# Postponed-layernorm ViT layer: a third buffer for h times C, transposes first in TensorE's step, the second image's projections over free banks, dummy matmuls at the end

## The chip, the cores and the metric

One core of one Trainium2 chip. The metric is the device time of one execution in microseconds (us), as the median of three runs. One of the executions was profiled; the trace and its rows are from that one.

## The reference, cut to what matters

Four images of 1024 tokens with 64 features go through three blocks in fp32: retention (scores weighted with a fixed 1024x1024 matrix, PReLU), a selective state scan, and a two-layer mixture of experts, with a layer norm behind the second and the third.

```python
# retention, per image
q, k, v = x @ Wq + bq, x @ Wk + bk, x @ Wv + bv
y = ((d_gamma * (q @ k.T)) @ v) @ Wo + bo
h = where(y >= 0, y, prelu_a * y)
# state scan: 128 channels, 16 states
x_main, x_gate = split(h @ W_in + b_in)
x_conv = silu(x_main @ W_conv + b_conv)
B, C = split(x_conv @ W_bc + b_bc);  dt = softplus(x_conv @ W_dt + b_dt)
h_state = exp(dt * A) * h_state + dt * B * x_conv      # along the 1024 tokens
y = (h_state * C).sum(states)
h = layernorm(h + (y * silu(x_gate)) @ W_out + b_out)
# experts: each group of 64 tokens has one routed expert of 16, and a shared one
f = relu(h @ Wi.T + bi)
for l in 0, 1:  f = relu(shared_l(f) + expert_l(f) + f)
h = layernorm(h + f @ Wo.T + bo)
```

## The kernel before, in words

Everything is written out by hand, engine by engine, with semaphores; no scheduler reorders anything. Features or channels lie on the partitions and tokens along the free axis, in fp32. PSUM is divided into five named parts: `acc_y` (two banks, the sum of h times C over the states, transposed), `slot` (two banks, named `decay` in the trace), `work` (two banks), `acc_r` (one) and `tail` (one).

Every engine runs the same double loop: phases p = -1 to 5, and in each 16 steps n, one per state of the scan (`PHASES`, `step_of`). In a phase, image p is scanned (state number k = 16 p + n), image p + 1, called head, goes through retention in steps 0 to 8 and through its conv, gate, B, C and step-size products in steps 9 to 13, and image p - 1 goes through its layer norms and expert products (`last_part`, 19 steps, the last three in the next phase). In steps 11 to 14 the queries, keys and values of the image after head are made. So phase -1 is the start, with image 0's retention alone, phases 0 to 3 scan images 0 to 3, and the rest is image 3's end alone.

One state k of the scan goes through four engines:
- ScalarE writes the decay exp(dt A) into `slot` (`fill_slot`, L653 through `decay_exp` L633), once scan k - 1 has read it.
- u times B: for 11 of the 16 states GpSimd makes it (`ub`, L811, three buffers); for states 0, 4, 8, 10 and 14 VectorE does it in PSUM (L907), where ScalarE has copied u (L651).
- VectorE scans along the tokens into one of three h buffers (L919).
- GpSimd multiplies h with the broadcast row C (`hc`, L820, two buffers, `weigh`).
- TensorE transposes hc in eight 128x128 pieces, adding them in `acc_y` (`states_out`, L500), two steps later.

In GpSimd's step n stand hc(k-1) and then ub(k+1). The B and C rows come from DRAM, 512 KB each as each partition gets a copy, through SyncE's queue: three b_row and four c_row buffers, loaded three steps ahead (`load_b`, `load_c`); the group weights of the expert products (`load_group`) and the output stand in the same queue.

TensorE's step n holds, in this order: tail parts marked EARLY; scores(n+1) and retention(n) for n < 8; at step 9 the conv product (L468, needs the finished h of retention) and the gate product (L477, needs ScalarE to have read the conv product out of `work`); at step 10 the products out of xc for B and C (L484) and for the step sizes (L490); then states_out(k-2); then a side projection (steps 11 to 14: q, first keys, values, second keys, each through `acc_r`, evicted by ScalarE, L667 to L673); then scores(0) of the next image at step 15; then tail parts marked LATE. The expert products of an image are four such parts (L563 for the bias, L568 for 8 groups): layer 1 for the two halves at steps 8 and 9, layer 2 at 11 and 12. VectorE evicts them (L972) in the steps that DVE_TAIL names. In the last image's end TensorE is alone, and `tail` and the first bank of `work` alternate.

At the start TensorE first multiplies zeros (L391), then the folded weights (L394 to L396), the queries, keys and values of image 0 (L404, L400, L410), then scores and retention.

## Time and profile before

| | us |
|---|---|
| median of three runs (lowest, highest) | 401.34 (395.81, 404.02) |
| the profiled execution | 401.9 |
| its span from first to last instruction | 400.1 |
| busy: TensorE matmuls / weight loads | 304.3 / 174.2 |
| busy: VectorE, ScalarE, GpSimd | 251.7, 175.0, 262.2 |
| mean granted TensorE clock, share of full speed | 0.805 |

The profile names the engines PE (TensorE matmuls), PEld (its weight loads), DVE (VectorE), ACT (ScalarE), POOL (GpSimd), SP (SyncE). A row of the groups of instructions gives, for a line and an operation, how often it ran, its busy time and mean duration, and the idle time of its engine just before it with what ended that. Busy matmul time is modelled, as matmuls are pipelined. The granted clock has two levels, 1.2 and 2.4 GHz, shown as 0.50 and 1.00 of full speed; a value between them is a mean over a stretch. An fp32 matmul appears as two records.

### The profile page before, as it was taken

Reading aid. Unit: us, or ns where it says so; the run is one execution under the profiler, and the core shown is the slowest. Engines: PE = TensorE matmul, PEld = TensorE weight load, DVE = VectorE, ACT = ScalarE, POOL = GpSimd, SP = SyncE. Lnnn points to the kernel's source line nnn. Section 1 sums busy time; section 2 is a strip of 40 time slices with the busy share of each in tenths; the row PEclk is TensorE's granted clock in tenths of the full one; section 3 lists DMA queues with packets and bytes.
Section 4 is the critical chain, followed back from the end, with each engine's and each line's share of the span. In section 5 each row is a group of like instructions: output and inputs, shape, how many; then the busy total and the mean of one; then the engine's idle time right before and its main releaser. Section 6 shows DMA issues by size and latency. Waiting matters only on the chain.

```text
span 400.1 us, 4140 instructions
## 1 busy us (share of the span) xinstructions
PE 304.3 (76%) x1368; PEld 174.2 (44%) x1368; DVE 251.7 (63%) x221; ACT 175.0 (44%) x209; POOL 262.2 (66%) x116
## 2 busy tenths in 40 slices
PE   8995779756686889699796997667655786956793
PEld 5321413322352434365742444456443375731771
DVE  3556268977388799752949988649667667640020
ACT  2019233347744336746363356863553533333003
POOL 0062219993998899746778799486999979840000
PEclk9999558995987999758689999896759586696556
DMA  7930837776569789953657998765699998313201
GB/s 262 422 116 13 313 111 280 242 244 240 183 223 260 274 270 328 274 193 141 209 185 228 273 298 302 240 214 202 220 302 283 323 317 280 107 26 98 61 2 26
DMA packets 42998, 85.87 MB, mean 215 GB/s; under 512 B 7904, under 2 KB 24800, under 8 KB 42720
## 3 DMA queue, kind: packets, MB, share of 16 engines
q1 hardware_dynamic: 42576, 84.43, 63.6%
q10 hardware_dynamic: 400, 1.17, 1.0%
q8 instruction: 11, 0.18, 0.2%
q14 instruction: 11, 0.09, 0.1%
HBM read 75.62 MB, written 1.57 MB: 193 GB/s over the span
## 4 chain that ended last, share of the span: by engine, by line
PE 35%; POOL 22%; DVE 19%; issue 10%; ACT 8%; DMA 3%; SPq 1%; POOLq 1%; DVEq 0%; ACTq 0%
POOL ub L811 12%; DVE h L919 11%; POOL hc L820 10%; PE acc_y L500 7%; PE tail L568 5%; PE acc_r L457 3%; PE work L448 3%; DVE decay L907 2%; DVE mixed L937 2%; DMA b_row<-bc_dram 2%; PE tail L522 2%; PE work L568 2%; PE tail L553 1%; PE tail L544 1%; PE work L490 1%
## 5 line engine op out<-in xcount | busy, mean ns | idle before, releaser
L820 POOL TENSOR_TENSOR hc<-h,c_row 128x1024 f32<-128x1024 f32 x64 | 151.8, 2372 | 55.5 <-PE acc_y L500 42.2
L919 DVE TENSOR_TENSOR_SCAN h<-decay,ub 128x1024 f32<-128x1024 f32 x44 | 100.8, 2290 | 49.1 <-POOL ub L811 41.6
L811 POOL TENSOR_TENSOR ub<-u,b_row 128x1024 f32<-128x1024 f32 x44 | 103.9, 2362 | 14.3 <-DMA b_row<-bc_dram 14.3
L633 ACT ACTIVATE decay<-delta,neg_a 128x1024 f32<-128x1024 f32 x44 | 49.2, 1119 | 96.6 <-DVE h L919 96.6
L500 PEld LDWEIGHTS acc_y<-pack,hc 128*128 128x128 f32 x512 | 68.1, 162 | 51.4 <-issue 30.3
L500 PE MATMUL acc_y<-pack,hc 128*128 128x128 f32 x512 | 81.9, 312 | 8.8 <-POOL hc L820 8.6
L937 DVE TENSOR_TENSOR mixed<-gam,work 128x512 f32<-128x512 f32 x56 | 35.6, 676 | 17.3 <-PE work L448 16.5
L919 DVE TENSOR_TENSOR_SCAN h<-decay_own,decay 128x1024 f32<-128x1024 f32 x20 | 45.7, 2286 | 0.7
L448 PE MATMUL work<-q,kT 64*128 64x512 f32 x112 | 35.5, 713 | 13.8 <-DVE mixed L937 11.0
L568 PEld LDWEIGHTS tail<-f,group_w 128*128 128x128 f32 x224 | 39.3, 263 | 1.0
L457 PE MATMUL acc_r<-mixed,v_sb 128*64 128x512 f32 x128 | 37.2, 662 | 1.7 <-DVE mixed L937 1.7
L568 PE MATMUL tail<-f,group_w 128*128 128x64 f32 x224 | 38.0, 344 | 0.0
L907 DVE TENSOR_TENSOR decay<-decay,b_row 128x1024 f32<-128x1024 f32 x20 | 24.6, 1230 | 14.3 <-ACT decay L651 14.3
L651 ACT ACTIVATE decay<-u 128x1024 f32<-128x1024 f32 x20 | 20.5, 1027 | 28.1 <-DVE h L919 28.1
L448 PEld LDWEIGHTS work<-q,kT 64*128 64x128 f32 x112 | 9.4, 204 | 31.9 <-DVE mixed L937 23.1
L633 ACT ACTIVATE decay_own<-delta,neg_a 128x1024 f32<-128x1024 f32 x20 | 22.7, 1136 | 0.0
L972 DVE TENSOR_SCALAR f<-tail 128x512 f32<-128x512 f32 x14 | 9.6, 686 | 17.1 <-PE tail L568 16.8
L563 PE MATMUL tail<-onehot,bias_w 96*128 96x512 bf16 x14 | 7.0, 503 | 15.8 <-DVE f L972 12.6
L797 POOL TENSOR_TENSOR expert_w<-expert_w 128x2048 f32<-128x2048 f32 x2 | 9.0, 4518 | 15.2 <-DMA expert_w<-routed_w 15.2
L457 PEld LDWEIGHTS acc_r<-mixed,v_sb 128*64 128x64 f32 x128 | 6.6, 141 | 28.0 <-issue 18.9
L732 ACT ACTIVATE ln_q<-tail,b_c 128x512 f32<-128x512 f32 x8 | 5.4, 678 | 26.6 <-PE tail L544 26.6
L400 PE MATMUL acc_r<-x_in,pack 128*128 128x512 f32 x12 | 9.0, 843 | 7.7 <-ACT q L667 6.5
(134 smaller groups left out, 297.3 us busy)
## 6 DMA issues: line engine op xcount, KB each, us to landing
b_row<-bc_dram SPq DMA_DIRECT2D x64, 512.0 KB, 5.0
c_row<-bc_dram SPq DMA_DIRECT2D x64, 512.0 KB, 5.1
group_w<-expert_w SPq DMA_DIRECT2D x64, 128.0 KB, 3.8
gam<-gammaT SPq DMA_DIRECT2D x8, 512.0 KB, 10.3
expert_w<-routed_w SPq DMA_DIRECT2D x1, 2048.0 KB, 18.1
x_in<-xT SPq DMA_DIRECT2D x4, 256.0 KB, 5.7
out<-res SPq DMA_DIRECT2D x8, 128.0 KB, 3.1
pack<-packed ACTq DMA_DIRECT2D x1, 788.0 KB, 6.6
```

The source lines that it names most:

```text
L448: nc.tensor.matmul(pair[:, i * HALF:(i + 1) * HALF], kT[D * i:D * i + D, j * P:(j + 1) * P], q2[D * i:D * i + D, :], start=True, stop=True ...
L457: mm = nc.tensor.matmul(acc_r[D * i:D * i + D, :], v_sb[:, j, :], mixed[:, j % 2, i * HALF:(i + 1) * HALF], start=(j == 0), stop=(j == TIL ...
L500: mm = nc.tensor.matmul(acc_y[:, c * P:(c + 1) * P], hc[:, k % 2, c * P:(c + 1) * P], ident, start=(n == 0 and c % 4 == 0), stop=(n == STA ...
L568: mm = nc.tensor.matmul(bank[:, (g % 8) * GROUP:(g % 8 + 1) * GROUP], group_w[:, g, layer, :], f[:, g * GROUP:(g + 1) * GROUP], start=Fals ...
L633: nc.scalar.activation(target, delta[:, b % 2, :], ACT.Exp, scale=neg_a[:, n:n + 1])\
L651: nc.scalar.activation(slot[:, :], u[:, b % 2, :], ACT.Copy).then_inc(u_copied, 1)
L811: nc.gpsimd.tensor_tensor(ub[:, j % 3, :], u[:, b % 2, :], b_row[:, k % 3, :], ALU.mult)\
L820: nc.gpsimd.tensor_tensor(hc[:, k % 2, :], h[:, k % 3, :], c_row[:, k % 4, :], ALU.mult)\
L907: nc.vector.tensor_tensor(slot[:, :], slot[:, :], b_row[:, k % 3, :], ALU.mult).then_inc(ub_own, 1)
L919: nc.vector.tensor_tensor_scan(h[:, k % 3, :], factor, term, 0.0, ALU.mult, ALU.add).then_inc(scan_done, 1)
L937: nc.vector.tensor_tensor(mixed[:, j % 2, at], gam[:, j, at], pair[:, at], ALU.mult).then_inc(read, 1)
L972: nc.vector.tensor_scalar(f[:, i * HALF:(i + 1) * HALF], bank[:, :], 0.0, None, ALU.max)\
```

## The change

- hc has three buffers in place of two, c_row three in place of four; C rows are loaded two steps ahead in place of three. The hc of state k waits for the transposes of k - 3.
- TensorE's step: states_out comes right behind scores and retention. The conv product follows it at step 9, the products out of xc at step 10 and the side projections too; the gate product is last in step 9, behind the LATE parts.
- The projections of the second image (made while image 0 is head) no longer alternate with ScalarE in `acc_r`: queries go to `acc_r`, both key halves to the two banks of `slot`, values to `acc_r`; VectorE evicts all four. ScalarE's first use of `slot` waits for that.
- Start: the folded weights come behind the keys, image 0's values behind scores(0, 0).
- Dummy matmuls of 256 columns into `acc_r` (or `slot`) that nobody reads: two at step 8 of phase -1; four ahead of each of the last two states_out; in image 3's end as WARM_AT says.
- VectorE evicts the second half of expert layer 1 at step 11 in place of 10.

```diff
-DVE_TAIL = {2: USE_YT, 3: USE_YT + 1, 6: USE_VAR1, 8: USE_L1, 10: USE_L1 + 1, 12: USE_L2, 13: USE_L2 + 1, 16: USE_VAR2}
+DVE_TAIL = {2: USE_YT, 3: USE_YT + 1, 6: USE_VAR1, 8: USE_L1, 11: USE_L1 + 1, 12: USE_L2, 13: USE_L2 + 1, 16: USE_VAR2}
...
+WARM_AT = {2: 1, 4: 2, 5: 4, 7: 1, 12: 1, 14: 2, 15: 4}
...
-        c_row = sb("c_row", [P, 4, T])
+        c_row = sb("c_row", [P, 3, T])
...
-        hc = sb("hc", [P, 2, T])
+        hc = sb("hc", [P, 3, T])
...
-                if k >= 4:
-                    sp.wait_ge(hc_ready, k - 3)
+                if k >= 3:
+                    sp.wait_ge(hc_ready, k - 2)
...
-                        load_c(k + 3)
+                    if scanned(k + 2):
+                        load_c(k + 2)
...
+            def keep_warm(bank, times):
+
+                for _ in range(times):
+                    nc.tensor.matmul(bank[:, 0:2 * INNER], gam[:, 0, 0:P], gam[:, 0, 0:2 * INNER], start=True, stop=True)
...
+                folded_weights()
+
+            def first_values():
                 pe.wait_ge(s_wvo, 1)
                 values(slot[:, 0:HALF]).then_inc(first_full, 1)
+
+            def next_projections():
+
+                pe.wait_ge(side_read, 1)
+                pe.wait_ge(s_x, 32)
+                queries(acc_r).then_inc(next_full, 1)
+                pe.wait_ge(slot_read, 10)
+                keys(0, slot[:, 0:HALF]).then_inc(next_full, 1)
+                keys(1, slot[:, HALF:T]).then_inc(next_full, 1)
+                pe.wait_ge(next_read, 1)
+                values(acc_r).then_inc(next_full, 1)
...
-                    if head is not None:
-                        if n + 1 < TILES:
-                            scores(head, n + 1)
-                        if n < TILES:
-                            retention(head, n)
-                        if n == 9:
-                            conv_product(head)
-                            gate_product(head)
-                        if n == 10:
-                            from_xc(head)
+                    if head is not None and n + 1 < TILES:
+                        scores(head, n + 1)
+                    if head is not None and n < TILES:
+                        retention(head, n)
+                    if p == IMAGES and n < 2:
+                        pe.wait_ge(side_read, side_use(IMAGES - 1, SIDE_BC) + 1)
+                        keep_warm(acc_r, 4)
                     if scanned(k - 2):
                         states_out(k - 2)
-                    if following is not None and n in SIDE_AT:
+                    if head is not None and n == 9:
+                        conv_product(head)
+                    if head is not None and n == 10:
+                        from_xc(head)
+                    if head == 0 and n == 11:
+                        next_projections()
+                    if following is not None and head > 0 and n in SIDE_AT:
                         side_projection(head, SIDE_AT[n])
                     if following is not None and n == STEPS - 1:
                         scores(following, 0)
                     for b, m in last:
                         last_part(b, m, LATE)
+                        if b == IMAGES - 1:
+                            keep_warm(acc_r, WARM_AT.get(m, 0))
+                    if head is not None and n == 9:
+                        gate_product(head)
...
+                else:
+                    act.wait_ge(next_read, 3)
...
-                if k >= 2:
-                    pool.wait_ge(hc_used, k - 1)
+                if k >= 3:
+                    pool.wait_ge(hc_used, k - 2)
...
+                    if head == 0 and n == 11:
+                        next_evictions((0, 1, 2))
...
+                        if head == 0:
+                            next_evictions((3,))
```

TensorE around step 9 of image 1's scan (image 0 in its tail, image 2 the head), before; the acc_y rows are states_out, the tail rows an expert product:

```order
L568 MATMUL tail<-f,group_w 128x64 x8
L468 MATMUL work<-hT,w_mc 128x512 x2
L477 MATMUL work<-hT,pack 128x512 x2
L500 MATMUL acc_y<-pack,hc 128x128 x8
L563 MATMUL tail<-onehot,bias_w 128x512
L568 MATMUL tail<-f,group_w 128x64 x8
L484 MATMUL acc_r<-mixed,pack 32x256 x4
L490 MATMUL work<-mixed,pack 128x512 x2
L500 MATMUL acc_y<-pack,hc 128x128 x16
```

The same place in the changed kernel (L499 conv, L508 gate, L531 states_out, L515 and L521 out of xc):

```order
L599 MATMUL tail<-f,group_w 128x64 x8
L531 MATMUL acc_y<-pack,hc 128x128 x8
L499 MATMUL work<-hT,w_mc 128x512 x2
L594 MATMUL tail<-onehot,bias_w 128x512
L599 MATMUL tail<-f,group_w 128x64 x8
L508 MATMUL work<-hT,pack 128x512 x2
L531 MATMUL acc_y<-pack,hc 128x128 x8
L515 MATMUL acc_r<-mixed,pack 32x256 x4
L521 MATMUL work<-mixed,pack 128x512 x2
L531 MATMUL acc_y<-pack,hc 128x128 x8
```

State 7's transposes moved ahead of the conv product, state 8's ahead of the products out of xc, and the gate product behind the second expert product.

TensorE at the end of phase -1, before: the second image's queries (L404), keys (L400), values (L410), keys, and its first scores:

```order
L490 MATMUL work<-mixed,pack 128x512 x2
L404 MATMUL acc_r<-x_in,pack 64x512 x2
L400 MATMUL acc_r<-x_in,pack 128x512
L410 MATMUL acc_r<-wvo,x_in 128x64 x8
L400 MATMUL acc_r<-x_in,pack 128x512
L448 MATMUL work<-q,kT 128x512 x4
```

The same in the changed kernel:

```order
L521 MATMUL work<-mixed,pack 128x512 x2
L419 MATMUL acc_r<-x_in,pack 64x512 x2
L415 MATMUL decay<-x_in,pack 128x512 x2
L425 MATMUL acc_r<-wvo,x_in 128x64 x8
L479 MATMUL work<-q,kT 128x512 x4
```

The keys go into `decay` (the slot bank) together, and the values come last.

TensorE at the end of image 3's scan, before and then after; L412 is a dummy:

```order
L549 MATMUL tail<-ln_q,pack 128x512
L500 MATMUL acc_y<-pack,hc 128x128 x16
L574 MATMUL tail<-pack,ln_y 128x128 x4
L539 MATMUL tail<-pack,y_t 128x128 x4
L539 MATMUL work<-pack,y_t 128x128 x4
```

```order
L580 MATMUL tail<-ln_q,pack 128x512
L412 MATMUL acc_r<-gam 128x256 x4
L531 MATMUL acc_y<-pack,hc 128x128 x8
L412 MATMUL acc_r<-gam 128x256 x4
L531 MATMUL acc_y<-pack,hc 128x128 x8
L605 MATMUL tail<-pack,ln_y 128x128 x4
L570 MATMUL tail<-pack,y_t 128x128 x4
L570 MATMUL work<-pack,y_t 128x128 x4
L412 MATMUL acc_r<-gam 128x256
```

Four dummies now stand ahead of each of the last two sets of transposes, and the rows of image 2 (L605) stand behind them.

## Rows read from the trace of the kernel before

**Rows 1.** Groups of instructions: line, engine, tiles, count | busy us, mean ns | idle before, releaser
```profile
L820 POOL TENSOR_TENSOR hc<-h,c_row 128x1024 f32<-128x1024 f32 x64 | 151.8, 2372 | 55.5 <-PE acc_y L500 42.2
```
**Rows 2.** Windows, from first hc to first hc, images 0 to 3; columns first
```profile
core 0: us, PE busy (x) PEld busy (x) DVE busy (x) ACT busy (x) POOL busy (x), PEclk, DMA share, GB/s
58.28:131.65 73.37, 52.23 (x232) 25.09 (x232) 57.44 (x44) 36.76 (x41) 63.68 (x28) 0.83 0.72 241
131.65:213.04 81.39, 70.96 (x332) 40.54 (x332) 57.18 (x47) 41.82 (x51) 62.94 (x28) 0.83 0.69 229
213.04:289.76 76.72, 58.84 (x308) 35.60 (x308) 59.03 (x48) 41.55 (x49) 62.91 (x28) 0.90 0.78 251
289.76:354.87 65.11, 45.17 (x220) 33.62 (x220) 44.74 (x28) 28.20 (x31) 60.37 (x26) 0.72 0.77 248
```
**Rows 3.** Waits of GpSimd in these four windows: us in total, times, longest
```profile
POOL hc L820 <- PE acc_y L500: 9.1, 2, 6.6
...
POOL hc L820 <- PE acc_y L500: 19.6, 7, 6.6
...
POOL hc L820 <- PE acc_y L500: 13.6, 6, 6.0
...
POOL hc L820 <- PE acc_y L500: 2.4, 2, 1.8
```
**Rows 4.** Timeline of TensorE, image 1: start us, us, line, tiles [idle before]
```profile
165.59 1.97 PE L468 MATMUL work<-hT,w_mc 64*128 64x512 f32 x4 [0.35 <-DVE hT L942]
169.74 2.08 PE L477 MATMUL work<-hT,pack 64*128 64x512 f32 x4 [2.18 <-ACT mixed L692]
...
173.94 3.51 PE L568 MATMUL tail<-f,group_w 128*128 128x64 f32 x16
...
185.46 1.90 PE L568 MATMUL tail<-f,group_w 128*128 128x64 f32 x16
```
**Rows 5.** Timelines of VectorE and GpSimd in the same place
```profile
166.13 2.29 DVE L919 TENSOR_TENSOR_SCAN h<-decay,ub 128x1024 f32<-128x1024 f32 x1
...
171.91 2.29 DVE L919 TENSOR_TENSOR_SCAN h<-decay_own,decay 128x1024 f32<-128x1024 f32 x1
...
173.89 2.36 POOL L820 TENSOR_TENSOR hc<-h,c_row 128x1024 f32<-128x1024 f32 x1 [6.57 <-PE acc_y L500]
```
**Rows 6.** Windows in the second half of image 1's scan, columns as in rows 2
```profile
167.60:183.00 15.40, 13.26 (x47) 8.50 (x48) 7.32 (x5) 9.16 (x13) 4.68 (x2) 0.51 0.59 197
...
193.00:201.00 8.00, 8.00 (x41) 8.00 (x40) 7.43 (x5) 1.33 (x2) 5.04 (x3) 0.50 0.61 204
```
**Rows 7.** Timelines of TensorE and VectorE, end of phase -1
```profile
41.30 2.08 PE L400 MATMUL acc_r<-x_in,pack 128*128 128x512 f32 x2 [3.87 <-ACT q L667]
...
40.79 1.29 DVE L950 TENSOR_TENSOR delta<-work,delta 128x512 f32<-128x512 f32 x2 [4.18 <-ACT delta L718]
42.23 1.23 DVE L957 TENSOR_TENSOR u<-delta,mixed 128x1024 f32<-128x1024 f32 x1
...
55.91 2.29 DVE L919 TENSOR_TENSOR_SCAN h<-decay_own,decay 128x1024 f32<-128x1024 f32 x1
```
**Rows 8.** The chain that ended last, a piece of it: start us, us
```profile
40.07 6.89 DMA b_row<-bc_dram
```
**Rows 9.** Timelines of TensorE and VectorE at the start
```profile
1.19 4.45 PE L391 MATMUL decay<-kT 128*128 128x256 f32 x10 [1.19 <-DVE kT L835]
...
12.35 1.28 DVE L937 TENSOR_TENSOR mixed<-gam,work 128x512 f32<-128x512 f32 x2 [0.44 <-PE work L448]
```
**Rows 10.** Timeline at the end, TensorE and SyncE's queue
```profile
352.47 1.09 PE L500 MATMUL acc_y<-pack,hc 128*128 128x128 f32 x8 [0.69 <-POOL hc L820]
...
354.92 1.09 PE L500 MATMUL acc_y<-pack,hc 128*128 128x128 f32 x8 [1.35 <-POOL hc L820]
...
358.98 15.56 SPq L352 DMA_DIRECT2D group_w<-expert_w  x12
...
376.21 0.58 PE L563 MATMUL work<-onehot,bias_w 96*128 96x512 bf16 x1 [2.01 <-DMA group_w<-expert_w]
```
**Rows 11.** Window at the end, columns as in rows 2
```profile
376.20:380.20 4.00, 3.99 (x18) 3.91 (x19) 0.06 (x1) 0.00 (x0) 0.00 (x0) 0.50 0.00 0
```

More of the change, by code:

```diff
@@ L219, in vit_layer @@
         scan_done = sem("scan_done")
-        c_loaded = [sem(f"c_row_loaded_{i}") for i in range(4)]
+        c_loaded = [sem(f"c_row_loaded_{i}") for i in range(3)]
         hc_ready = sem("hc_ready")
@@ L772, in _ @@
                             softplus_curve(head)
[L773 removed]
+                    if following is not None and head > 0 and n in SIDE_AT:
                         side_eviction(head, SIDE_AT[n])
```

50 lines of the change are left out of this document (35 added, 15 removed).

## The prediction

> **What bounds the kernel now.** I read the groups of instructions first, to see which engine carries the state scan and what it waits for. The costliest group is GpSimd's product hc = h times C, 64 times 2,372 ns. It has 55.5 us of idle time before it, and 42.2 us of that was ended by TensorE's transposes into acc_y [rows 1]: GpSimd wants to write one of two hc buffers, and TensorE has not read it yet.
>
> Next I cut the time at the starts of the first hc of each image, 58.28, 131.65, 213.04 and 289.76 us, up to the end of the last hc at 354.87, and asked for busy times [rows 2]. GpSimd is busy for 63.68, 62.94, 62.91 and 60.37 us in stretches of 73.37, 81.39, 76.72 and 65.11 us. It has the most even load, and its own work (about 63 us per image) is the floor. In the second stretch TensorE is busy for 70.96 us, above GpSimd; in the others it is below. VectorE has 57 to 59 us per image with attention beside it.
>
> Then the waits of GpSimd for TensorE, one stretch at a time [rows 3]: 9.1, 19.6, 13.6 and 2.4 us. They sum to 44.7 against 42.2 in rows 1, since the 2.5 us up to the cut at 131.65 are counted on both sides; I leave them with image 0, and image 1 keeps 17.1. The long ones sit at step 9 of an image. In image 1's scan TensorE stands with the conv product at 165.59, then the gate product at 169.74 (it waits there for ScalarE's silu of the conv product), and only then come the transposes of state 7 [rows 4]. Their end releases the hc of state 9 at 173.89, after 6.57 us of waiting [rows 5]. TensorE runs its matmuls in the order of the program, so a transpose whose data was long there stood behind a product that waited.
>
> What lies outside the four stretches: 58.3 us of start, in which the first scan begins only at 55.91 [rows 7], and 45 us of end, where TensorE works alone at a granted clock of 0.50 [rows 11].
>
> **The change, part by part.** All sums are made against the profiled execution: span 400.1 us, time 401.9, so 1.8 around it. The median of the three runs is 401.34, practically the same.
>
> (a) Second image's projections. Now they go q, first half of keys, values, second half of keys through the one bank acc_r, each evicted by ScalarE, which first does the softplus. The first key half starts only at 41.30, after 3.87 us of waiting for ScalarE, and takes 2.08, the duration of the low clock; the values, the other key half and the scores follow in turn, and the first scan is at 55.91 [rows 7]. After: q into acc_r, both key halves into the free slot bank, values into acc_r as soon as VectorE has copied q. VectorE was idle for the 4.18 us up to 40.79 anyway [rows 7]. Queries start at 36.9 (0.6 late by (b)). My estimate at the full clock, where each of these takes half of what it takes in rows 7: q to 38.0, keys to 40.0, values to 41.9 (1.0, 2.0, 1.9 us). VectorE then adds delta, makes u (42.23 now, 1.23 us [rows 7]; 0.6 later by (b)), copies v to 44.7. The scores come at 44.8, the first mixed product ends at about 46.8, or at 47.6 if the clock has fallen by then; the B multiply takes 1.24. The B row is no limit: the landing that ends the 6.89 us piece at 46.96 [rows 8] is that of the second B row, and it now stands ahead of the first C row in SyncE's queue. First scan at 48.1 to 48.8. Gain 7.5 us taken; from 4 (a cold TensorE and a wait at the new copies) to 9.
>
> (b) Start of the program. The folded weights move behind the first keys, so queries start 0.9 earlier, but the values now stand behind scores(0,0) and the folded weights' copy, and VectorE must evict them before it makes the first mixed product. Now that starts at 12.35 [rows 9]; I get 13.1. Cost 0.6, between -1 and +1; it is already in (a)'s 7.5. The two dummies at step 8 fill a gap of 1.0 us: nothing.
>
> (c) Three hc buffers and transposes first. A product hc(k) now waits for the transposes of k-3 in place of k-2, which is one step (4.7 us) of slack; and states 7 and 8 no longer stand behind the conv product and the block of products out of xc. (The gate product still stands ahead of state 8.) This can give back the waits of rows 3, less what comes next. Next at step 9: hc(9) cannot start before scan 9 ends at 168.42, 1.1 us after GpSimd is free, and hc(10) not before scan 10, which ends at 174.20 [rows 5], again 1.1 us after GpSimd would have finished hc(9) and ub(11). These 2.2 us stay in each of three images, since scan 10 waits for ScalarE, which I leave where it is.
> Image 0: 9.1 - 2.2 = 6.9; 6.5 taken, from 4 to 7.
> Image 1: 17.1 - 2.2 = 14.9 by GpSimd, but TensorE has 70.96 us of work there, so at the present clock (0.83) at most 81.39 - 70.96 = 10.4. TensorE never ran without gaps, so I take 6.5, from 2 to 14 (above 10.4 only with a better clock).
> Image 2: 13.6 - 2.2 = 11.4 by GpSimd; TensorE has 58.84, so it is no limit. I take 8, since the gate product now stands behind the group product of the second half of layer 1 (1.90 at the full clock, 3.51 at the low one [rows 4]); ScalarE's gates, its table load and the next decay follow it. From 4 to 11.4.
> Image 3: 2.4 at most; 2 taken, from 0.
> The eviction of that group product moves from step 10 to 11 on VectorE. That frees scan 11 from waiting for it, and makes layer 2's product later by a scan (2.3 us), on a TensorE that stood idle there for its input.
>
> (d) One C buffer fewer. The C row is issued when the third product before it has ended. Between them stand two hc and two or three ub of 2.36, 9.4 to 11.8 us, at least 7.1 around an image's start; a row of this size landed in 6.89 with three others ahead of it [rows 8], and about 2 us of issue of group weights may come on top. Hidden: 0 taken. Up to 1 us at each of the four image starts if not.
>
> (e) Dummies at the end. Five dummies at the start took 4.45 us [rows 9], 0.89 each at the low clock, so about 0.45 at full. Four stand ahead of each of the last two sets of transposes, 3.6 us in all. TensorE was idle for 0.69 and 1.35 us there, waiting for hc [rows 10], so the very last set starts 3.6 - 2.0 = 1.6 later. That moves the rows of image 2, and behind these SyncE holds twelve loads of group weights, 358.98 to 374.5 [rows 10]; the second group product started at 376.21 on their landing. So whatever the dummies win before that (1.6 us in the first group product, the like in the layer norm) ends in a longer wait at that place. Behind it three group products at the low clock, as now; one dummy at 0.9 on the path; a few tenths back in the last transposes. Sum +2, from -4 (the clock comes back) to +4.
> Here a rule and a row disagree. The row: from 376.20 to 380.20 TensorE is busy for 3.99 of 4.00 us and the granted clock stays at 0.50 [rows 11], and it had been idle before that. The Trainium skill (TensorE: Matmul & The Clock Gate, "What's actually happening") says that the throttled state is the default and that activity releases it. The idle part agrees, the busy part does not, as the profile counts busy. By the rule the products behind the first one would run at full clock, three times 1.6 us less, and the end would be -3 in place of +2; I go by the row.
>
> Sum: -7.5 - 6.5 - 6.5 - 8 - 2 + 2 = -28.5. 401.9 - 28.5 = 373.4, forecast 373 us. Its own range is 363 to 384.
>
> **The rivals.**
> B, TensorE has room after all and the clock stays up: then the waits come back whole, 7.5 + 6.9 + 14.9 + 11.4 + 2.4 + 3 = 46.1, 356 us. For it: in the second stretch the weight loads are busy for only 40.54 of 81.39 us, and the stretches at 0.51 and 0.50 [rows 6] begin after waits which this change removes. Against it: TensorE busy 8.00 of 8.00 us there. The Trainium skill (Perfetto Trace Analysis, "Identifying the Most-Contended Engine") says that matmul busy time is no measure of headroom and that weight load time is a better one; by it image 1 would not be bound by TensorE, and the time would be this rival's.
> C, the wait changes its name: GpSimd no longer waits for TensorE but for scans, and these for ScalarE's decay, which stands behind gates and softplus, whose products TensorE makes later than now. Then about a third of the waits comes back, 3 + 4 + 4 + 1 = 12, with 7.5 from the start and +2 at the end: 384 us; with a poorer start 388. For it: decay waits for scans and scans for ub in a ring, so no part has much slack. Against it: in rows 3 the waits are single and long, 6.6 us, where a ring would take them back in steps of 1 to 2.
> D, slower: TensorE drops to the low clock in images 1 and 2. Image 1's work is 70.96 x 0.83 = 59 us at full clock, 118 at the low one; image 2's 58.84 x 0.90 = 53 and 106. With two thirds of the work at the low clock they take 98 and 88 us, so +17 and +11, and with 7.5 + 6.5 won in front, 2 in image 3 and +2 at the end: 416 us. It decides from about half of the work at the low clock, where the sum of all is nil. For it: 0.50 while fully busy in rows 6. Against it: the change removes idle time of TensorE, and the clock was 0.83 and 0.90 over these stretches.
> That the dummies do not hold the clock is already in the forecast.
>
> **How the numbers follow.** Forecast 0.64, B 0.12, C 0.18, D 0.06. The low end takes in half of B, the high end C: 359 to 388. A measurement of this kernel can tell 2% or about 8 us. Forecast, B and C are all faster by more than that (0.94, less 0.01 for a C with a bad start); D is split between within 2% and slower: 0.93, 0.04, 0.03.
>
> **What would show it.** In the new profile: the first scan at about 48.5 us; waits of hc for acc_y under 10 us in sum; image stretches of about 67, 75, 69 and 63 us; the last transposes 1 to 2 us behind their hc; the second group product of the end still waiting for the group weights, with a clock of 0.50 behind it. Wrong if the stretches are as before and only the releaser has changed (C), if image 1 is at 64 to 66 (B), or if the clock in images 1 and 2 is below 0.7 (D).

## The result and the profile after

The changed kernel takes 372.66 us (four runs, 371.45 to 374.7); the kernel before, run beside it, took 398.87 (395.81 to 404.02). The ratio is 0.937, with an interval from 0.926 to 0.948; the run of 404.02 us, in a slower state of the chip, is left out of it, so it isn't the quotient of the two medians. The profiled execution took 371.63 us, with a span of 369.8 and a mean granted clock of 0.866, against 401.9, 400.1 and 0.805 before. The forecast was 373 us.

The group of the product hc in the new profile, which answers to [rows 1]:

```profile
L862 POOL TENSOR_TENSOR hc<-h,c_row 128x1024 f32<-128x1024 f32 x64 | 153.6, 2400 | 23.3 <-DVE h L974 22.4
```

The wait for TensorE (42.2 us) is gone. What is left is a wait for VectorE's scans, 22.4 us. The four stretches from first hc to first hc, and to the end of the last one, as in [rows 2]:

```profile
51.53:118.64 67.11, 48.94 (x222) 22.22 (x220) 55.03 (x42) 35.51 (x41) 63.69 (x27) 0.83 0.76 257
118.64:186.94 68.30, 61.55 (x342) 34.07 (x340) 59.44 (x49) 42.61 (x52) 63.85 (x28) 0.98 0.86 280
186.94:258.85 71.91, 58.74 (x308) 33.99 (x308) 58.92 (x48) 41.00 (x49) 63.76 (x28) 0.91 0.83 268
258.85:323.59 64.74, 45.44 (x229) 34.86 (x230) 44.77 (x28) 28.30 (x31) 60.45 (x26) 0.74 0.80 259
```

GpSimd's busy time is within 1 us of what it was (63.7, 63.9, 63.8, 60.5 us), and the stretches have come down to 3.4 to 8.2 us above it. Its waits inside each of the four windows (total, times, longest), which answer to [rows 3]:

```profile
POOL hc L862 <- DVE h L974: 6.1, 4, 3.5
...
POOL hc L862 <- DVE h L974: 4.8, 7, 1.5
...
POOL hc L862 <- DVE h L974: 8.1, 6, 4.3
...
POOL hc L862 <- DVE h L974: 3.5, 3, 1.9
```

Against the terms of the prediction, all in us and from one profiled execution each (how much such a stretch differs between executions of the same code is told further down, under image 2):

| part | before | after | gain | predicted |
|---|---|---|---|---|
| up to the first hc | 58.28 | 51.53 | 6.75 | 7.5 |
| image 0 | 73.37 | 67.11 | 6.3 | 6.5 |
| image 1 | 81.39 | 68.30 | 13.1 | 6.5 |
| image 2 | 76.72 | 71.91 | 4.8 | 8 |
| image 3 | 65.11 | 64.74 | 0.4 | 2 |
| from the last hc to the end | 45.2 | 46.2 | -1.0 | -2 |
| sum | | | 30.3 | 28.5 |

The start, first TensorE's timeline, as in [rows 7]:

```profile
37.43 1.08 PE L419 MATMUL acc_r<-x_in,pack 128*64 128x512 f32 x4 [0.39 <-ACT mixed L707]
38.44 1.98 PE L415 MATMUL decay<-x_in,pack 128*128 128x512 f32 x4
40.26 1.90 PE L425 MATMUL acc_r<-wvo,x_in 128*128 128x64 f32 x16
45.28 1.36 PE L479 MATMUL work<-q,kT 64*128 64x512 f32 x4 [3.12 <-DVE v_sb L907]
```

VectorE's timeline there and at the beginning, as in [rows 9]:

```profile
13.44 1.27 DVE L992 TENSOR_TENSOR mixed<-gam,work 128x512 f32<-128x512 f32 x2
...
31.11 0.75 DVE L997 SCALAR_TENSOR_TENSOR hT<-acc_r,neg_ba,hT 128x512 f32<-128x512 f32 x1 [2.46 <-ACT acc_r L724]
...
49.17 2.29 DVE L974 TENSOR_TENSOR_SCAN h<-decay_own,decay 128x1024 f32<-128x1024 f32 x1
```

Projections run one behind the other; then TensorE waits 3.12 us for VectorE's copy of v. The first scan starts at 49.17 in place of 55.91. The first mixed product starts at 13.44, 1.1 later than before.

The end, TensorE, as in [rows 10]; L412 is a dummy:

```profile
320.98 1.89 PE L412 MATMUL acc_r<-gam 128*128 128x256 f32 x8
322.71 1.04 PE L531 MATMUL acc_y<-pack,hc 128*128 128x128 f32 x8
323.58 1.89 PE L412 MATMUL acc_r<-gam 128*128 128x256 f32 x8
325.31 1.04 PE L531 MATMUL acc_y<-pack,hc 128*128 128x128 f32 x8
...
340.00 1.89 PE L599 MATMUL tail<-f,group_w 128*128 128x64 f32 x16
346.54 0.59 PE L594 MATMUL work<-onehot,bias_w 96*128 96x512 bf16 x1 [4.64 <-DMA group_w<-expert_w]
346.91 3.52 PE L599 MATMUL work<-f,group_w 128*128 128x64 f32 x16
```

And two windows there, as in [rows 11]:

```profile
342.00:346.50 4.50, 0.00 (x0) 0.00 (x0) 0.62 (x1) 0.00 (x0) 0.00 (x0) 0.61 0.31 90
346.50:350.50 4.00, 3.96 (x18) 3.91 (x19) 0.03 (x1) 0.00 (x0) 0.00 (x0) 0.50 0.01 4
```

The first group product runs at the full clock (1.89 us), then TensorE waits 4.64 us for weights, and the products behind take 3.52 us at a granted clock of 0.50.

### The profile page after: what moved, and what is told of

It reads as the page before. It is cut to its first block, busy times and chain, and to the rows that moved or that the text cites. A ratio compares the mean times of both kernels' runs of the same rounds, so it can differ in the third digit from the quotient of the medians.

```text
span 369.8 us, 4241 instructions
## 1 busy us (share of the span) xinstructions
PE 292.9 (79%) x1418; PEld 168.5 (46%) x1418; DVE 253.4 (69%) x225; ACT 172.0 (47%) x205; POOL 264.1 (71%) x116
## 4 chain that ended last, share of the span: by engine, by line
PE 31%; DVE 24%; ACT 13%; POOL 12%; issue 11%; SPq 4%; DMA 4%; DVEq 0%; POOLq 0%; ACTq 0%
DVE h L974 14%; POOL ub L853 7%; PE work L479 6%; DVE decay L962 5%; POOL hc L862 5%; PE acc_r L488 5%; PE acc_y L531 5%; DMA c_row<-bc_dram 3%; PE tail L599 3%; ACT decay L693 2%; DVE mixed L992 2%; SPq L357 2%; ACT decay L673 2%; PE work L599 2%; PE acc_r L412 1%
## 5 line engine op out<-in xcount | busy, mean ns | idle before, releaser
L862 POOL TENSOR_TENSOR hc<-h,c_row 128x1024 f32<-128x1024 f32 x64 | 153.6, 2400 | 23.3 <-DVE h L974 22.4
L853 POOL TENSOR_TENSOR ub<-u,b_row 128x1024 f32<-128x1024 f32 x44 | 103.8, 2358 | 13.1 <-DMA b_row<-bc_dram 13.1
L531 PEld LDWEIGHTS acc_y<-pack,hc 128*128 128x128 f32 x512 | 63.4, 154 | 44.7 <-issue 30.2
L531 PE MATMUL acc_y<-pack,hc 128*128 128x128 f32 x512 | 76.7, 298 | 5.8 <-POOL hc L862 5.8
L479 PE MATMUL work<-q,kT 64*128 64x512 f32 x112 | 37.3, 745 | 15.4 <-DVE mixed L992 10.2
L488 PE MATMUL acc_r<-mixed,v_sb 128*64 128x512 f32 x128 | 38.2, 679 | 0.9 <-DVE mixed L992 0.8
L599 PEld LDWEIGHTS tail<-f,group_w 128*128 128x128 f32 x224 | 34.1, 232 | 0.9
L599 PE MATMUL tail<-f,group_w 128*128 128x64 f32 x224 | 32.7, 310 | 0.0
L570 PE MATMUL tail<-pack,y_t 128*128 128x128 f32 x28 | 5.6, 337 | 10.2 <-ACT y_t L765 10.2
```

The lines of the kernel that those rows point to most:

```text
L479: nc.tensor.matmul(pair[:, i * HALF:(i + 1) * HALF], kT[D * i:D * i + D, j * P:(j + 1) * P], q2[D * i:D * i + D, :], start=True, stop=True ...
L488: mm = nc.tensor.matmul(acc_r[D * i:D * i + D, :], v_sb[:, j, :], mixed[:, j % 2, i * HALF:(i + 1) * HALF], start=(j == 0), stop=(j == TIL ...
L531: mm = nc.tensor.matmul(acc_y[:, c * P:(c + 1) * P], hc[:, k % 3, c * P:(c + 1) * P], ident, start=(n == 0 and c % 4 == 0), stop=(n == STA ...
L599: mm = nc.tensor.matmul(bank[:, (g % 8) * GROUP:(g % 8 + 1) * GROUP], group_w[:, g, layer, :], f[:, g * GROUP:(g + 1) * GROUP], start=Fals ...
L853: nc.gpsimd.tensor_tensor(ub[:, j % 3, :], u[:, b % 2, :], b_row[:, k % 3, :], ALU.mult)\
L862: nc.gpsimd.tensor_tensor(hc[:, k % 3, :], h[:, k % 3, :], c_row[:, k % 3, :], ALU.mult)\
```

## The experiments

Medians are compared with the changed kernel's 372.66 us, or with the run named; ratios are against the kernel before, with their intervals. The kernel before was run again beside each set of experiments and gave medians from 396.5 to 401.2 us, so a difference of a microsecond or two between medians of different sets shows nothing by itself.

### Buffers alone, order alone, both

e1_buffers, on the kernel before:

```diff
-        c_row = sb("c_row", [P, 4, T])
+        c_row = sb("c_row", [P, 3, T])
...
-        hc = sb("hc", [P, 2, T])
+        hc = sb("hc", [P, 3, T])
...
-                        load_c(k + 3)
+                    if scanned(k + 2):
+                        load_c(k + 2)
...
-                if k >= 2:
-                    pool.wait_ge(hc_used, k - 1)
+                if k >= 3:
+                    pool.wait_ge(hc_used, k - 2)
```

e2_order, on the kernel before:

```diff
-                        if n == 9:
-                            conv_product(head)
-                            gate_product(head)
-                        if n == 10:
-                            from_xc(head)
...
                     if scanned(k - 2):
                         states_out(k - 2)
+                    if head is not None and n == 9:
+                        conv_product(head)
+                    if head is not None and n == 10:
+                        from_xc(head)
...
                         last_part(b, m, LATE)
+                    if head is not None and n == 9:
+                        gate_product(head)
```

It also has VectorE's eviction of the second half of expert layer 1 at step 11. e12_both has the two edits together.

> The kernel before, with three hc buffers and three c_row buffers alone; TensorE's order, the start and the end as they were. Theory 1 (the buffer carries the gain): one step of slack, 4.7 us, covers nearly all of the waits in rows 3, of which the longest is 6.6, so GpSimd waits for acc_y under 6 us in sum in place of 42.2, and about 20 us go: ratio to the kernel before 0.945 to 0.955. Theory 2 (the order carries it): the transposes of state 7 still stand behind the gate product, so the long waits shrink only by 4.7 each, and the rest of the wait turns up as a wait for scans: ratio 0.97 to 0.98.

> The kernel before, with the new order of TensorE's step alone (transposes right behind retention, gate product last in step 9, second half of expert layer 1 evicted a step later); two hc buffers, start and end as they were. Theory 1: only the waits at step 9 go (6.6, 6.6, 6.0); the 1 to 5 us ones at other steps stay, since the transposes stand at the same place there: acc_y waits fall from 42 to about 22 us, ratio 0.97 to 0.98. Theory 2 (order carries it): waits under 10 us, ratio 0.95.

> The two together, on the kernel before; start and end as they were. Both theories: what is left is the start (6.75 us in the traces) and the end (1.0 us lost), so the ratio is that of the changed kernel plus 0.014, 0.945 to 0.955. If the two overlap, it equals the better of the two alone; if they add, it is their product.

| | us (lowest, highest) | ratio | images 0, 1, 2, 3 |
|---|---|---|---|
| e1_buffers | 380.01 (379.58, 382.96) | 0.950 [0.942, 0.959] | 67.16, 70.63, 72.13, 65.9 |
| e2_order | 382.25 (378.02, 384.58) | 0.950 [0.937, 0.963] | 68.76, 67.89, 73.63, 66.6 |
| e12_both | 378.57 (375.85, 379.38) | 0.946 [0.936, 0.955] | 67.11, 69.19, 70.64, 66.3 |

Waits of GpSimd over the whole span, with the buffers alone:

```profile
POOL hc L821 <- DVE h L920: 31.6, 22, 10.3
...
POOL hc L821 <- PE acc_y L501: 1.9, 2, 1.1
```

The same view with the order alone:

```profile
POOL hc L820 <- DVE h L919: 21.5, 12, 9.1
...
POOL hc L820 <- PE acc_y L500: 13.8, 12, 3.0
```

The third buffer takes the wait for acc_y from 42.2 to 1.9 us and gives 5% alone. The order alone leaves 13.8 us of the wait, now in pieces of at most 3.0 where 6.6 was the longest, and gives as much time, as far as the intervals tell. I had expected a ratio of 0.97 to 0.98 of it. Together they give hardly more than either (0.946, with intervals that overlap): they remove the same wait, once by slack and once by its cause, and what remains is GpSimd's own work and the scans.

### The second image's projections as before, and the start as before

e3_old_projections, on the changed kernel (TensorE's part; VectorE's and ScalarE's go with it):

```diff
-                    if head == 0 and n == 11:
-                        next_projections()
-                    if following is not None and head > 0 and n in SIDE_AT:
+                    if following is not None and n in SIDE_AT:
```

e5_old_start, on the changed kernel:

```diff
-                folded_weights()
...
+            folded_weights()
             first_projections()
+            first_values()
             scores(0, 0)
-            first_values()
```

> The changed kernel with the second image's projections as before, one at a time through acc_r with ScalarE's evictions. Theory: the first hc starts 6.75 us later (58.3 in place of 51.5) and all behind it is shifted by that: ratio to the kernel before 0.949 to 0.955, that is 1.2 to 1.8% above the changed kernel. Rival (the gain of the start is eaten by the scan stage, since GpSimd is bound there by scans and the C rows come later): under 0.5% above.

> The changed kernel with the start as before: folded weights, queries, keys, values, then scores. In the changed kernel the first finished h of image 0 comes at 31.11 against 30.04 us before. Theory: that 1.1 us goes through to the end, so this is 1 us faster than the changed kernel: 0.934 against 0.937, ratio within the interval of it, and the first hc 1.1 us earlier. Rival: the 1.1 us is another thing (the load of the first constants, which landed 0.4 later in that trace): then 0 to 0.4 us.

e3_old_projections: 380.91 us (377.63 to 381.34), ratio 0.958 [0.953, 0.963], span 375.8 against 369.8. TensorE's first key half, which waits for ScalarE again:

```profile
42.52 2.08 PE L412 MATMUL acc_r<-x_in,pack 128*128 128x512 f32 x2 [3.87 <-ACT q L700]
```

VectorE's first scan in this run:

```profile
57.13 2.29 DVE L965 TENSOR_TENSOR_SCAN h<-decay_own,decay 128x1024 f32<-128x1024 f32 x1
```

The gain of the start goes through to the end: 8 us in the scan's start, 6.0 in the span of the two profiled executions, 8.3 in the medians. The 6.75 us that I expected lie between these.

e5_old_start: 372.34 us (371.25 to 373.11), ratio 0.938 [0.934, 0.942], span 369.9. VectorE in this run:

```profile
29.98 0.75 DVE L997 SCALAR_TENSOR_TENSOR hT<-acc_r,neg_ba,hT 128x512 f32<-128x512 f32 x1 [2.46 <-ACT acc_r L724]
...
48.80 2.29 DVE L974 TENSOR_TENSOR_SCAN h<-decay_own,decay 128x1024 f32<-128x1024 f32 x1
```

With the old start image 0's h is ready 1.13 us sooner (29.98 against 31.11), but the scan only 0.37. In the time nothing can be seen (372.34 against 372.66), so the microsecond that I expected to go through to the end did not. The 0.37 us is small against what executions with the same start differ by: the first hc stands at 51.53 us in the changed kernel, and at 52.64, 53.05, 52.50 and 52.06 in e6_early_loads, e12_fewer_dummies, e11_yt_late and e15_yg_later, which have its start unchanged.

### The dummies and the wait for the group weights

The four kernels of this part differ in two things: whether the dummies behind the start are there, and when SyncE issues image 3's sixteen group weights. In the changed kernel four of them stand ahead of the store of image 2's output and twelve behind it; the edit puts all sixteen ahead of it:

e6_early_loads, on the changed kernel:

```diff
-                        if m < 8:
+                        if b == ALONE and m == 0:
+                            for g in range(GROUPS_IMG):
+                                load_group(b, g)
+                        elif b < ALONE and m < 8:
```

e4_no_dummies, on the changed kernel, and e8_early_no_dummies, on e6_early_loads:

```diff
-                    if p == IMAGES and n < 2:
-                        pe.wait_ge(side_read, side_use(IMAGES - 1, SIDE_BC) + 1)
-                        keep_warm(acc_r, 4)
...
-                        if b == IMAGES - 1:
-                            keep_warm(acc_r, WARM_AT.get(m, 0))
...
-                        keep_warm(slot, 2)
```

e13_before_early is the kernel before with the edit of e6_early_loads.

> The changed kernel without any of its dummy matmuls but the five at the very start. Theory 1 (the dummies win nothing since SyncE's group loads gate the second group product): the very last transposes start up to 1.6 us earlier, the group loads with them, and one dummy less stands in front of the last residual product: 1 to 2 us faster than the changed kernel, ratio to the kernel before 0.932 to 0.936. Rival (the dummies hold the clock in the end): the layer norm and the last products are slower by 2 to 4 us: 0.942 to 0.948.

> The changed kernel, but SyncE issues all 16 group weights of image 3 ahead of image 2's output, instead of 12 of them behind it; the dummies stay. Theory (these loads gate the second group product, and TensorE loses the clock while it waits 4.6 us for them): the wait goes, 4.6 us, and the four group products run at 1.9 in place of 3.5 us, 3 times 1.6, with about 1 more in the residual product behind them: 8 to 10 us less than the changed kernel, ratio 0.911 to 0.918. Rival (the group products lose the clock by themselves, as the 0.50 while fully busy suggests): 4.6 us less, ratio 0.925.

> The same early loads, but without the dummies. Theory (the dummies pay only where nothing else ends later): the wait for the loads was 1.8 us there, and the group products stay at 3.5 us each: 1.8 us less than without dummies, 371 us, ratio 0.928; so the dummies are then worth 5 to 7 us. Rival: the clock comes back by itself once the products stand back to back, then as fast as with dummies or faster by the 1.1 us that those cost ahead of the last transposes.

> The kernel before, with one edit: SyncE issues the sixteen group weights of image 3 ahead of the store of image 2's output. It asks whether what the changed kernel gains by this (372.7 to 361.0) is there for any kernel or only where dummies keep the clock up. Theory 1 (only the wait for the weights goes, 2.01 us here, since the group products run at the low clock anyway): 2 us less than before, ratio 0.99 to 1.00, group products at 3.5 us. Theory 2 (the idle time at the wait is what brings the clock down in this kernel too): group products at 1.9 us, 8 to 10 us less, ratio 0.975 to 0.98.

| us (lowest, highest), ratio | twelve loads behind the output | all ahead of it |
|---|---|---|
| with dummies | 372.66, 0.937 [0.926, 0.948] | 361.04 (360.59, 362.43), 0.910 [0.907, 0.914] |
| without | 372.94 (371.9, 373.07), 0.932 [0.923, 0.941] | 370.86 (369.63, 373.22), 0.935 [0.930, 0.940] |
| kernel before | 396.5 to 401.2, the medians beside these runs | 398.15 (395.11, 401.14), 0.998 [0.992, 1.003] |

The dummies alone give nothing: neither the 1 to 2 us that I expected to win without them nor the 2 to 4 us of the rival came. Without them (e4_no_dummies) the group products all take 3.5 us:

```profile
342.22 3.51 PE L599 MATMUL tail<-f,group_w 128*128 128x64 f32 x16
347.51 0.59 PE L594 MATMUL work<-onehot,bias_w 96*128 96x512 bf16 x1 [1.77 <-DMA group_w<-expert_w]
347.89 3.52 PE L599 MATMUL work<-f,group_w 128*128 128x64 f32 x16
```

The early loads alone give 2 us in the medians (370.86 against 372.94), which is about the length of the wait, but the ranges and the intervals of the two overlap, so this isn't told from nothing; what the profile does show is that the wait of 1.77 us is gone and that the products stay at 3.5 us. In the kernel before their effect can't be told from nothing (0.998): its wait was 2.01 us [rows 10], the profile of e13_before_early no longer has it, and the group products stay at 3.5 us. Dummies and early loads together give 11.6 us, and of these 9.8 are between the two kernels with early loads, where neither ranges nor intervals overlap. TensorE's timeline at the end of e6_early_loads:

```profile
340.68 1.89 PE L602 MATMUL tail<-f,group_w 128*128 128x64 f32 x16
...
342.63 1.90 PE L602 MATMUL work<-f,group_w 128*128 128x64 f32 x16
...
346.53 1.89 PE L602 MATMUL work<-f,group_w 128*128 128x64 f32 x16
```

Two windows of the same run, in which these products lie:

```profile
340.00:344.00 4.00, 3.96 (x33) 3.53 (x33) 0.69 (x1) 0.94 (x2) 0.00 (x0) 1.00 0.01 4
344.00:348.00 4.00, 4.00 (x37) 3.94 (x37) 1.38 (x2) 0.00 (x0) 0.00 (x0) 1.00 0.00 0
```

No wait, and all four products at 1.9 us. The same instructions, as densely packed as behind the wait in the changed kernel (matmul busy 3.96 of 4.00 us in both), have a granted clock of 1.00 here and 0.50 there. What differs is what TensorE did before: here it came in busy and at 1.00, there it had been idle for 4.64 us. e8_early_no_dummies is the third case: it has no wait either, but TensorE came in at 0.50 after work with gaps, and all four products take 3.5 us:

```profile
338.00:342.00 4.00, 3.31 (x14) 2.06 (x11) 0.00 (x0) 1.27 (x2) 0.00 (x0) 0.50 0.00 0
342.00:346.00 4.00, 4.00 (x20) 3.91 (x20) 0.69 (x1) 0.00 (x0) 0.00 (x0) 0.50 0.00 0
```

So these products kept whichever of the two levels they came in at.

### Without the eight dummies ahead of the last transposes

e12_fewer_dummies, on e6_early_loads:

```diff
-                    if p == IMAGES and n < 2:
-                        pe.wait_ge(side_read, side_use(IMAGES - 1, SIDE_BC) + 1)
-                        keep_warm(acc_r, 4)
```

> The changed kernel with the early group loads, without the two sets of four dummies ahead of the last two states_out; the dummies behind stay. It asks for the term of 1.6 us that I put on these eight. Theory 1 (they only delay the last transposes, and the clock is full there without them): the very last set starts right behind its hc in place of 1.7 us behind it, the end gets shorter by 1 to 1.7 us, the four group products stay at 1.9 us each: 359.4 to 360.2. Theory 2 (without them the clock falls before the first layer norm, and the later dummies do not bring it back in time): some of the group products take 3.5 us, time 362 to 370.

359.41 us (357.57 to 360.11), ratio 0.901 [0.895, 0.908]: 1.6 us less than with them (361.04), the figure that (e) put on them. The two ranges just don't overlap and the intervals do, and the two spans are 0.9 us apart (358.3 and 359.2), so the size is uncertain. The last transposes wait for their hc again, and the group products stay at 1.9 us:

```profile
326.54 1.09 PE L534 MATMUL acc_y<-pack,hc 128*128 128x128 f32 x8 [1.63 <-POOL hc L862]
...
341.77 1.90 PE L602 MATMUL work<-f,group_w 128*128 128x64 f32 x16
```

### What holds image 2 up

In the changed kernel GpSimd waits 4.28 us for scan 35. TensorE's timeline there:

```profile
189.02 1.73 PE L479 MATMUL work<-q,kT 64*128 64x512 f32 x4 [2.60 <-DVE mixed L992]
...
197.07 2.08 PE L479 MATMUL work<-q,kT 64*128 64x512 f32 x4
```

VectorE's timeline there:

```profile
197.17 0.69 DVE L1022 TENSOR_TENSOR f<-gate,tail 128x512 f32<-128x512 f32 x1 [2.48 <-PE tail L570]
199.25 1.28 DVE L992 TENSOR_TENSOR mixed<-gam,work 128x512 f32<-128x512 f32 x2 [1.39 <-PE work L479]
200.45 2.28 DVE L974 TENSOR_TENSOR_SCAN h<-decay,ub 128x1024 f32<-128x1024 f32 x1
```

VectorE has the product of gate and y_t ahead of scan 35 and waits for its transposes; TensorE has these ahead of the next scores. Two runs change these orders.

e11_yt_late, on e6_early_loads, in TensorE's table:

```diff
-    (2, EARLY): ((USE_YT, WHOLE),), (2, LATE): ((USE_YT + 1, WHOLE),), (3, LATE): ((USE_OUT1, RESIDUAL),),
+    (2, LATE): ((USE_YT, WHOLE), (USE_YT + 1, WHOLE)), (3, LATE): ((USE_OUT1, RESIDUAL),),
```

e15_yg_later, on e12_fewer_dummies (359.41 us), in TensorE's table and VectorE's:

```diff
-    (2, EARLY): ((USE_YT, WHOLE),), (2, LATE): ((USE_YT + 1, WHOLE),), (3, LATE): ((USE_OUT1, RESIDUAL),),
-    (4, LATE): ((USE_OUT1, REST),), (5, LATE): ((USE_VAR1, WHOLE),), (6, LATE): ((USE_F0, WHOLE),),
+    (2, LATE): ((USE_YT, WHOLE),), (3, LATE): ((USE_YT + 1, WHOLE),),
+    (4, LATE): ((USE_OUT1, RESIDUAL), (USE_OUT1, REST)), (5, LATE): ((USE_VAR1, WHOLE),), (6, LATE): ((USE_F0, WHOLE),),
...
-DVE_TAIL = {2: USE_YT, 3: USE_YT + 1, 6: USE_VAR1, 8: USE_L1, 11: USE_L1 + 1, 12: USE_L2, 13: USE_L2 + 1, 16: USE_VAR2}
+DVE_TAIL = {3: USE_YT, 4: USE_YT + 1, 6: USE_VAR1, 8: USE_L1, 11: USE_L1 + 1, 12: USE_L2, 13: USE_L2 + 1, 16: USE_VAR2}
```

> The changed kernel with the early group loads (361.04 us), and one line of TensorE's table moved: the two transposes of y_t of an image stand behind states_out of step 2 in place of ahead of scores(3). It asks what is left of the term for image 2, forecast 8 us and measured 4.8: there GpSimd waits 4.28 us for the scan of state 35 at 202.81, VectorE stood 2.48 us for y_t's transposes and then 1.39 us for the scores of the next tile, which TensorE makes behind these transposes. Theory 'order' (the term was too large since a second product stands in TensorE's order ahead of what the scan's engine needs): scores(3) and retention(2) go into the 1.92 us that TensorE idles for ScalarE's y_t, the wait of 1.39 us goes, the wait of hc at the start of image 2's scan falls from 4.3 (2.2 in the run with early loads) by 1.4 or more, and images 1 and 2 together take 1.5 to 4 us less: 357.5 to 359.5. Theory 'ring' (GpSimd, VectorE and ScalarE bind each other, and TensorE is not what is late): the wait moves to another scan, time within 1 us of 361. Against both: the transposes of state 16's hc and y_t now come later, and image 1's last products with them: up to 2 us slower.

> The kernel of e12_fewer_dummies (359.41 us), with the work on y_t at an image's start one step later on TensorE and on VectorE: transposes in the LATE parts of steps 2 and 3, the output product whole in step 4, VectorE's products of gate and y_t in steps 3 and 4, each behind that step's scan. It follows the run in which TensorE's order alone was changed: there VectorE still stood 1.49 us at the product of gate and y_t, with scan 35 behind it, and GpSimd's wait for scan 35 was 1.76 us. Theory 'VectorE's order' (scan 35 is late since VectorE takes the product of gate and y_t first): GpSimd's wait for the scan of state 35, 3.44 us at 203.16 in the run without these eight dummies, falls under 1 us, and image 2's stretch, 72.46 us there, to 70 or less: 356.5 to 358. Theory 'ring': the wait turns up at a later scan, or the output product's wait for VectorE holds TensorE and the scores of tile 5 up in turn: 359 to 361, and image 2's stretch stays above 71.

e11_yt_late: 360.85 us (359.32 to 362.88), ratio 0.906 [0.899, 0.913]; no difference from 361.04. The wait for scan 35 is 1.76 in place of 2.23 us, and image 2 took 70.01 in place of 70.34. The theory 'order' as I put it falls: with the scores made earlier, VectorE still stood 1.49 us at the product of gate and y_t, and the time stayed.

e15_yg_later: 356.32 us (354.62 to 358.04), ratio 0.894 [0.888, 0.900], 3.1 less than 359.41. All but one of its six times lie below all six of the other run's, though the two intervals overlap, so a gain is likely and its size open. The stretches of the two profiled executions are 66.64, 68.66, 70.66 and 65.0 us, against 67.16, 67.91, 72.46 and 65.9. So images 2 and 3 gained 1.8 and 0.9, image 1 lost 0.7, and the rest is in front. The wait for scan 35 fell from 3.44 to 2.24 us, not under 1 as expected, and image 2 ended just above my 70. What stands ahead of the scan is another thing now. TensorE's timeline in this run:

```profile
189.45 2.08 PE L482 MATMUL work<-q,kT 64*128 64x512 f32 x4 [2.60 <-DVE mixed L992]
191.46 1.97 PE L491 MATMUL acc_r<-mixed,v_sb 128*64 128x512 f32 x4
193.36 1.97 PE L534 MATMUL acc_y<-pack,hc 128*128 128x128 f32 x8
```

VectorE's timeline behind it:

```profile
197.13 1.28 DVE L992 TENSOR_TENSOR mixed<-gam,work 128x512 f32<-128x512 f32 x2 [2.01 <-PE work L482]
198.84 2.29 DVE L974 TENSOR_TENSOR_SCAN h<-decay,ub 128x1024 f32<-128x1024 f32 x1 [0.43 <-issue]
```

TensorE runs at the low clock here behind 2.60 us of idle time (2.08, 1.97 and 1.97 us), and VectorE waits 2.01 us for the scores.

Neither run settles the cause, as the place differs from execution to execution without any edit to it. Six of the kernels have the same instructions in the same order from image 0's scan to the end of image 2's, and differ only at the start or in image 3's end. In each of them TensorE stands idle there and then makes scores, retention and transposes:

| | idle, us | scores, retention, transposes, us | GpSimd's wait for scan 35, us | image 2, us |
|---|---|---|---|---|
| changed kernel | 2.60 | 1.73, 1.97, 1.19 | 4.28 | 71.91 |
| e5_old_start | 2.60 | 1.35, 1.98, 1.56 | 3.90 | 71.89 |
| e4_no_dummies | 2.60 | 1.13, 1.98, 1.77 | 3.79 | 71.92 |
| e12_fewer_dummies | 2.60 | 1.13, 1.65, 1.97 | 3.44 | 72.46 |
| e6_early_loads | 2.41 | 1.13, 1.08, 1.09 | 2.23 | 70.34 |
| e8_early_no_dummies | 2.60 | 1.13, 1.08, 1.09 | 1.34 | 69.02 |

In e6_early_loads the next scores, behind another 1.93 us of idle time, are slow (2.00 us); in e8_early_no_dummies the clock is up throughout:

```profile
191.30:200.20 8.90, 6.96 (x39) 3.45 (x40) 7.88 (x8) 4.93 (x5) 8.90 (x5) 1.00 0.90 251
```

So the wait for scan 35 goes with TensorE's clock at this place: 1.34 us where it stayed at 1.00, 3.4 to 4.3 where it fell among these three products. The 1.76 and 2.24 us of the two edited kernels and their 70.01 and 70.66 us for image 2 lie inside what the six differ by, and so the profiles don't show that either order made them.

## Why the prediction was right, and where its terms were not

The forecast of 373 us and its mechanisms hold: the time is 372.66, and the rivals B (356), C (384) and D (416) did not come. That it is met to half a microsecond is luck: two terms were mis-sized in opposite directions, image 1 by 6.6 us too little and image 2 by 3.2 too much, with smaller ones at the start, in image 3 and at the end.

**The start, (a) and (b).** 6.75 us came where 7.5 was taken. Queries started at 37.43, half a microsecond behind the 36.9 worked out, and the values ended at 42.2 against 41.9. The scores came 0.5 late (45.28 against 44.8), and they took 1.36 us, partly at the low clock, as the sentence on the first mixed product allowed; the scan started at 49.17 against 48.8 at most. In the four other executions with this start the first hc comes 0.5 to 1.5 us later still, so the start gives 5.2 to 6.75 us against the profile of before. e3_old_projections shows that it goes through to the end. The 0.6 us of (b) can't be told from nothing by e5_old_start.

**Image 0.** 6.3 against 6.5. The two waits that were expected at step 9 are in the trace, 1.18 us at 87.78 and 1.12 at 93.56, against two times 1.1.

**Image 1, the term that failed by size.** It gave 13.1, not 6.5 (inside its range of 2 to 14). I had capped it by TensorE's busy time of 70.96 us "at the present clock (0.83)". That busy time is no floor: it fell to 61.55 us as the mean clock in the stretch rose from 0.83 to 0.98. In the run with the order alone it was 59.39 us at 1.00, in the window of this image:

```profile
127.77:195.66 67.89, 59.39 (x332) 32.21 (x330) 57.69 (x47) 41.41 (x51) 63.13 (x27) 1.00 0.85 276
```

The gate product, at the low clock behind a wait of 2.18 us in [rows 4], takes 1.13 us behind a wait of 0.51 in the changed kernel, and the group product that took 3.51 takes 1.90. So the clock rose where the waits became short, and it was the low clock that had made TensorE look like the bound. That the shorter waits are what kept it up is read from these rows; no run changed the clock alone. In the six kernels of the table above image 1 took 67.9 to 69.7 us, so this term doesn't hang on one execution. This part of rival B came true: its 14.9 against 13.1. The Trainium skill (Perfetto Trace Analysis, "Identifying the Most-Contended Engine") says that weight load time, beside the work done, tells headroom better than matmul busy time; the trace agrees for this image, where weight loads were busy 40.54 of 81.39 us before.

**Image 2, the other one.** 4.8, not 8. The allowance for the gate product behind the group product was not the reason: the waits of that place are 1.16 and 1.09 us. The rest is the wait of 4.28 us for scan 35, of which I had nothing. In the trace of before GpSimd waited 0.76, 1.42 and 1.16 us for acc_y at this place, at 218.46, 224.55 and 228.07. This is rival C in small, a wait that changes its name, in one place only. What I had left out is that the clock can fall there: the six executions of the same code gave 4.3 to 7.7 us for this image, and the 7.7 belongs to the one with the clock up. The 8 us taken were thus about right for the waits, and too much by what the clock cost in the profiled execution. e11_yt_late and e15_yg_later don't show what VectorE's order has in it beside that; and why the clock fell in four of these executions and stayed up in e8_early_no_dummies, behind the same 2.60 us, stays open.

**Image 3** gave 0.4 of 2: its waits of 2.4 us for acc_y and 2.1 for scans became 3.5 for scans and 0.5 for a B row. **The C rows (d)** cost nothing: GpSimd never waited for c_row.

**The end, (e).** -1.0 against -2, as worked out: the last transposes 1.7 us behind their hc, then the wait of 4.64 us, 2.6 longer than before, that takes back what the first group product (1.89 in place of 3.51) and the layer norm won. By the Trainium skill (TensorE: Matmul & The Clock Gate, "What's actually happening") activity releases the throttle. I went by the row, rightly for this kernel: from 346.50 to 357.6 TensorE was busy throughout and the three group products took 3.5 us each. Behind them the clock did come back, while TensorE, no busier than before, made one dummy (L412) and the residual product (L553):

```profile
357.60:360.30 2.70, 2.70 (x6) 1.21 (x5) 0.69 (x1) 0.00 (x0) 0.00 (x0) 0.54 0.00 0
360.30:363.20 2.90, 2.90 (x11) 1.36 (x11) 0.00 (x0) 1.27 (x2) 0.00 (x0) 1.00 0.00 0
```

So the clock rose while TensorE was at work, as the rule has it, but the 11 us of group products ahead of that had not raised it. e6_early_loads shows the other half: the same products keep the full clock if TensorE reaches them at it.

**The two causes of (c)** I had treated as one term, and rightly so; but in what I expected of e1_buffers and e2_order I took the buffer for the main one. The order alone gives as much.

## What to carry to other kernels

A busy time read at a reduced clock is not a floor: if the change removes the idle time in front of that work, work out the floor at the full clock as well and let the range reach to it. Filling idle time to keep the clock up pays only once no longer wait follows in the same stretch; look for a transfer that the faster stretch will now run into (here nothing for the dummies alone, at most 2 us for the early loads alone, 11.6 for both). And two edits that remove the same wait don't add: price the wait, not the edits. Last, before a stretch of one profile is explained by an order of work, look at the same stretch in other executions of the same code: image 2 here took 69.0 to 72.5 us with nothing changed in it.

## What was not expected of the hardware

The granted clock depended on what had gone before, in both directions. Behind 4.64 us without a matmul, TensorE stayed at 0.50 for 11 us of uninterrupted group products; without that wait the same products ran at 1.00 throughout. At the start of image 2 the clock fell behind an idle time of 2.60 us in four executions of the same code, a little earlier or later in each, and stayed up behind the same 2.60 us in a fifth. So the length of the idle time alone doesn't decide it in these rows, and they are not enough for a rule.
